# Four-layer graph kernel: intermediates kept in PSUM, bias adds on GpSimd, the diagonal term on VectorE, and a new order of work

## What is computed

```python
# layer 0: attention, 12 heads, masked by adj     layer 3: attention, 12 heads, bias adj, then Wo
# layer 1, twice: h_lin = h @ W_lin.T + b_lin;  ctx = (exp(u)*adj / sum) @ h_lin;  h = relu(ln(ctx))
# layer 2, twice:
a = softmax(h @ h.T / sqrt(D));  delta = a * adj;  attn = delta / (sum(delta) + 1e-10)
hl, hs, hr = h @ wl.T + b_l, h @ ws.T + b_s, h @ wr.T + b_r
ctx = (attn * upper) @ hl + diagonal(attn)[..., None] * hs + (attn * lower) @ hr
h = relu((ctx - mean) / sqrt(var + 1e-12) * g + beta)
```

## Time and profile before

| | |
|---|---|
| median of 3 runs | 2933.51 us (2930.34 to 2935.92) |
| the profiled execution | 2933.42 us, of which the span from first to last instruction is 2931.7 us |
| PE busy | 2823.5 us, 96% |
| DVE busy | 2403.6 us, 82% |
| ACT busy | 1825.3 us, 62% |
| POOL (GpSimd) busy | 1349.7 us, 46% |
| mean granted TensorE clock | 0.988 |
| DMA transposes | 960, 15 per element |

### The profile page before, as it was taken

One profiled execution on the slowest core, in us unless ns is written; L12 is line 12 of the kernel. 1 busy time (PEld: TensorE's weight loads), 2 busy tenths in 40 slices (PEclk: granted clock), 3 DMA queues, 4 the chain that ended last, 5 costly groups with the idle time before them and its releaser, 6 DMA issues.

```text
span 2931.7 us, 93395 instructions
## 1 busy us (share of the span) xinstructions
PE 2823.5 (96%) x35008; PEld 2091.8 (71%) x35008; DVE 2403.6 (82%) x8566; ACT 1825.3 (62%) x4885; POOL 1349.7 (46%) x2571
## 2 busy tenths in 40 slices
PE   6899999999999999999999999999999999999996
PEld 4666767777777777777777777777777777777764
DVE  6867888788888888888888888888888878888767
ACT  5745566566666666666666666666666666665546
POOL 2334454354454454454454454454454445444545
PEclk9899999999999999999999999999999999999997
DMA  9414354344444444444454454444443444544325
GB/s 238 86 30 72 67 101 77 61 84 70 84 86 68 84 85 72 83 86 69 84 84 71 84 84 71 85 84 70 85 84 70 82 77 80 91 79 75 56 39 101
DMA packets 803991, 237.41 MB, mean 81 GB/s; under 512 B 771544, under 2 KB 803416, under 8 KB 803424
## 3 DMA queue, kind: packets, MB, share of 16 engines
q1 hardware_dynamic: 795808, 218.28, 42.3%
q10 hardware_dynamic: 7744, 13.17, 1.4%
HBM read 29.99 MB, written 12.58 MB: 15 GB/s over the span
## 4 chain that ended last, share of the span: by engine, by line
PE 76%; DMA 7%; DVE 6%; ACT 3%; POOL 3%; SPq 2%; issue 2%; ACTq 0%; DVEq 0%; POOLq 0%
PE bank L801 10%; PE bank L802 9%; PE bank L803 9%; PE bank L789 8%; PE bank L790 7%; PE bank L791 7%; PE bank L893 6%; DMA turned<-flat 6%; PE bank L838 4%; PE bank L807 3%; PE bank L886 2%; PE bank L823 2%; PE bank L825 2%; PE bank L824 2%; DVE score L974 2%
## 5 line engine op out<-in xcount | busy, mean ns | idle before, releaser
L789 PE MATMUL bank<-turned,w_hi 128*128 128x128 f16 x4608 | 817.2, 220 | 19.7 <-DMA turned<-flat 17.7
L790 PE MATMUL bank<-turned,w_hi 128*128 128x128 f16 x4608 | 816.4, 220 | 0.0
L791 PE MATMUL bank<-turned,w_lo 128*128 128x128 f16 x4608 | 816.3, 220 | 0.0
L801 PE MATMUL bank<-w_hi,turned 128*128 128x384 f16 x2112 | 692.4, 328 | 23.7 <-DVE w_lo L925 14.2
L802 PE MATMUL bank<-w_lo,turned 128*128 128x384 f16 x2112 | 691.0, 327 | 0.0
L803 PE MATMUL bank<-w_hi,turned 128*128 128x384 f16 x2112 | 690.8, 327 | 0.0
L716 ACT ACTIVATE score<-score,small 128x128 f32<-128x128 f32 x1536 | 500.9, 391 | 152.7 <-DVE small L980 138.0
L707 ACT ACTIVATE ab<-bank 128x384 f16<-128x384 f32 (+1 forms) x768 | 367.0, 484 | 254.3 <-PE bank L791 130.8
L609 POOL TENSOR_TENSOR flat<-score,flat 128x384 f16<-128x384 f32 x256 | 237.2, 927 | 613.6 <-ACT flat L722 613.0
L789 PEld LDWEIGHTS bank<-turned,w_hi 128*128 128x128 f16 x4608 | 453.8, 98 | 51.8 <-DMA turned<-flat 22.4
L790 PEld LDWEIGHTS bank<-turned,w_hi 128*128 128x128 f16 x4608 | 453.9, 99 | 18.6 <-issue 13.1
(11 more groups left out here) (116 smaller groups left out, 6559.0 us busy)
## 6 DMA issues: line engine op xcount, KB each, us to landing
turned<-flat SPq DMA_TRANSPOSE x960, 2.8
x<-x_dram SPq DMA_DIRECT2D x64, 192.0 KB, 2.4
out_dram<-score SPq DMA_DIRECT2D x64, 192.0 KB, 2.2
w_stage<-w_dram ACTq DMA_DIRECT2D x19, 576.0 KB, 5.6
adj<-adj_dram SPq DMA_DIRECT2D x64, 64.0 KB, 2.3
rows<-rows_dram ACTq DMA_DIRECT2D x1, 1920.0 KB, 9.3
turned<-bias_dram SPq DMA_DIRECT2D x4, 9.0 KB
beta<-beta_dram SPq DMA_DIRECT2D x1, 0.5 KB, 6.3
```

The lines of the kernel that those rows point to most:

```text
L789: pe.matmul(dst, lhsT=w_hi[:, w, k, cols], rhs=t_hi[u][:, k, :], start=(k == 0), stop=False)
L790: pe.matmul(dst, lhsT=w_hi[:, w, k, cols], rhs=t_lo[u][:, k, :], start=False, stop=False)
L791: last = pe.matmul(dst, lhsT=w_lo[:, w, k, cols], rhs=t_hi[u][:, k, :], start=False, stop=(k == DT - 1 and w not in BIAS_OF))
L801: pe.matmul(dst, lhsT=t_hi[u][:, k, :], rhs=w_hi[:, w, k, :], start=(k == 0), stop=False)
```

## The change

1. **Biases.** `BIAS_OF` keeps three biases (L0_Q, L0_K, L3_V). The other eight (weights 5, 8 and 9 to 14) are now added by a new POOL part `bias`: after ACT has copied the projection to SBUF, POOL adds a row of `rows` in place. `mix` waits for `biased` instead of ACT's copy.
2. **Diagonal.** `turn_delta` makes only the two triangles, and in an instruction of its own a per-node number, the diagonal. `mix` 2 and 3 issue two matmuls instead of three, and `inner` begins with one more DVE instruction: hs times the diagonal, added into the bank.
3. **PSUM.** `e` of `u_gcn` and `u_di`, and the results of `inner` and `gain`, stay in the PSUM bank in which PE made the product. The banks are handed on only after `delta_gcn`, `delta_di`, `turn` or `residual` has read them.
4. **Small parts.** The `TICK` copies go; `sums` on POOL takes two instructions instead of four.
5. **Memory and start.** The three weight staging tiles now lie in the tiles of the seventh unit, so element 6 is loaded only after all weights are split. `rows` comes in two loads. In `plan()`, the loads of weights 6 to 18 follow parts of ACT (`LOADED_AFTER`; the element that is furthest decides), DMA queues and a slow PE after a pause are part of the model, and transposes are taken to land after 3.60 instead of 3.15 us.
6. **Order.** All urgencies, durations and shifts are new; `PERIOD` is 41.981 instead of 43.452.

```diff
-BIAS_OF = {L0_Q: 0, L0_K: 1, 5: 2, 8: 3, 9: 4, 10: 5, 11: 6, 12: 7, 13: 8, 14: 9, L3_V: 10}
+BIAS_OF = {L0_Q: 0, L0_K: 1, L3_V: 2}
+ROW_OF = {5: 6, 8: 7, **{w: 3 + w for w in range(9, 15)}}
...
-    (PE, "mix", 2): (502.90, 2.010, 2.240, ((VECTOR, "turn_delta", 0), (SCALAR, "project", 9), (SCALAR, "project", 10), (SCALAR, "project", 11)), ()),
+    (PE, "mix", 2): (417.061, 1.340, 1.570, ((VECTOR, "turn_delta", 0), (POOL, "bias", 9), (POOL, "bias", 10), (POOL, "bias", 11)), ()),
...
+LOADED_AFTER = {6: ((SCALAR, "scores", 1),), 7: ((SCALAR, "scores", 2),), 8: ((SCALAR, "scores", 3),), 9: ((SCALAR, "turn", 1),), 10: ((SCALAR, "project", 3),), 11: ((SCALAR, "project", 4),), 12: ((SCALAR, "u_gcn", 0),), 13: ((SCALAR, "turn", 2),), 14: ((SCALAR, "project", 6),), 15: ((SCALAR, "norm", 1),), 16: ((SCALAR, "turn", 3),), 17: ((SCALAR, "u_di", 0),), 18: ((SCALAR, "turn", 4),)}
...
-           "turn_adj": lambda k: (SCALAR, "turn_adj", k), "u_gcn": lambda k: (VECTOR, "u_gcn", k),
-           "u_di": lambda k: (SCALAR, "u_di", k), "turn_delta": lambda k: (VECTOR, "turn_delta", k),
-           "mix": lambda k: (VECTOR, "inner", k)}
+           "turn_adj": lambda k: (SCALAR, "turn_adj", k), "u_gcn": lambda k: (VECTOR, "delta_gcn", k),
+           "u_di": lambda k: (VECTOR, "delta_di", k), "turn_delta": lambda k: (VECTOR, "turn_delta", k),
+           "mix": lambda k: ((VECTOR, "turn", 2), (VECTOR, "residual", 1), (VECTOR, "turn", 4), (VECTOR, "residual", 2))[k]}
...
+        w_stage = [last_unit[:, n * DT * D:(n + 1) * DT * D] for n in range(STAGES)]
...
+            def bias(i, w):
+                u = i % UNITS
+                pool.wait_ge(*proj_hi_done.at(i, "made", w))
...
+                made = proj[u][2 if w < 9 else (w - 9) % 3]
+                pool.tensor_tensor(made, made, rows[:, ROW_OF[w], :], ALU.add).then_inc(biased.of(i), 1)
...
                     for w in L2_W[k - 2]:
-                        pe.wait_ge(*proj_hi_done.at(i, "made", w))
+                        pe.wait_ge(*biased.at(i, "made", w))
                     pe.wait_ge(*mixed_out.at(i, "delta3", k - 2))
-                    for m in range(3):
-                        last = pe.matmul(made[:, 0:D], lhsT=delta3[u][:, m, :], rhs=proj[u][m], start=(m == 0), stop=(m == 2))
-                    last.then_inc(multiplied.of(i), 1)
+                    pe.matmul(made[:, 0:D], lhsT=triangles[u][:, 0, :], rhs=proj[u][0], start=True, stop=False)
+                    pe.matmul(made[:, 0:D], lhsT=triangles[u][:, 1, :], rhs=proj[u][2], start=False, stop=True)\
+                      .then_inc(multiplied.of(i), 1)
...
-                dve.tensor_tensor(delta3[u], bank("turn_delta", layer, i)[:, 0:N].unsqueeze(1).broadcast_to([128, 3, N]), tri[:, :, :], ALU.mult)\
+                dve.tensor_tensor_reduce(out=score[u][:, 2, :], in0=turned, in1=ident, scale=1.0, scalar=0.0, op0=ALU.mult,
+                                         op1=ALU.add, accum_out=col(u, DIAGONAL)).then_inc(numbers.of(i), 1)
+                dve.tensor_tensor(triangles[u], turned.unsqueeze(1).broadcast_to([128, 2, N]), tri[:, 0:2, :], ALU.mult)\
                    .then_inc(mixed_out.of(i), 1)
...
+                if k >= 2:
+                    dve.wait_ge(*numbers.at(i, "diagonal", k - 2))
+                    dve.scalar_tensor_tensor(made[:, 0:D], proj[u][1], col(u, DIAGONAL), made[:, 0:D], ALU.mult, ALU.add)\
+                       .then_inc(numbers.of(i), 1)
...
-                dve.scalar_tensor_tensor(zc[u], made[:, 0:D], mv[u][:, 0:1], rows[:, 2 * k, :], ALU.subtract, ALU.mult)\
+                dve.scalar_tensor_tensor(inner_of(i, k), made[:, 0:D], mv[u][:, 0:1], rows[:, GAIN_ROW[k], :], ALU.subtract, ALU.mult)\
...
-                dve.scalar_tensor_tensor(z[u], zc[u], col(u, GAIN if k < 2 else ROOT), rows[:, 2 * k + 1, :], ALU.mult, ALU.add)\
+                dve.scalar_tensor_tensor(inner_of(i, k), inner_of(i, k), col(u, GAIN if k < 2 else ROOT), rows[:, GAIN_ROW[k] + 1, :], ALU.mult, ALU.add)\
```

More of the change, by code:

```diff
@@ L233 @@
-    (SYNC, "turn", 5): (933.49, 1.240, 3.150, ((POOL, "turn", 5),), ()),
+    (PE, "turn_adj", 0): (0.000, 0.120, 0.380, ((VECTOR, "scores", 3),), ()),
+    (POOL, "turn", 0): (66.763, 0.868, 1.110, ((SCALAR, "turn", 0),), ()),
+    (PE, "mix", 1): (69.466, 0.700, 0.830, ((POOL, "bias", 8), (VECTOR, "delta_gcn", 1)), ()),
+    (POOL, "inner", 1): (73.012, 0.515, 0.765, ((VECTOR, "inner", 1),), ()),
+    (SCALAR, "turn", 0): (103.510, 0.412, 0.707, ((SYNC, "load", 0),), ()),
+    (VECTOR, "gain", 1): (107.515, 0.916, 1.240, ((POOL, "inner", 1),), ()),
@@ new lines @@
+    (POOL, "bias", 5): (478.539, 0.920, 1.200, ((SCALAR, "project", 5),), ()),
+    (PE, "project", 12): (480.991, 1.464, 1.644, ((SYNC, "turn", 4),), ()),
+    (PE, "project", 14): (483.572, 1.464, 1.644, ((SYNC, "turn", 4),), ()),
+    (POOL, "bias", 13): (485.571, 0.920, 1.200, ((SCALAR, "project", 13),), ()),
+    (PE, "scores", 7): (491.204, 0.300, 0.480, ((SCALAR, "scores", 6),), ()),
+    (VECTOR, "gain", 0): (491.504, 0.919, 1.243, ((POOL, "inner", 0),), ()),
+    (POOL, "sums", 0): (493.150, 0.441, 0.662, ((VECTOR, "delta_di", 0),), ()),
@@ L460, in bank, with e_of, inner_of @@
             return pool_of_banks[BANKS_AT[name, k, i][0][n]]
+        def e_of(i, name, layer):
+            return bank(name, layer, i)[:, 0:N]
+        def inner_of(i, k):
+            return bank("mix", k, i)[:, 0:D]
         def across(tile):
```

563 lines of the change are left out of this document (293 added, 270 removed).

## The result

The changed kernel takes 2813.17 us, the median of four runs (2807.87 to 2813.78), against 2934.72 for the kernel before (2930.34 to 2939.37). The ratio is 0.9582, with a 95% interval of 0.9562 to 0.9601. The forecast was 2780 with a range of 2735 to 2850. The direction and the range held; the gain came out as 122 us where 153 was forecast. The profiled execution took 2813.78 us, of which the span is 2812.0.

What follows compares the result with a forecast made beforehand. PE's issue was taken to bound the kernel: 2933.4 us less 166.7 of matmuls is 2766.7, plus 21 of waits in the middle, less 7 at the start, 2780.7, forecast 2780 us. Range 2735 to 2850.

Steps and rivals of the forecast that it cites:

- The work taken off PE: On PE, 512 bias matmuls (83.5 us) and 128 third matmuls of `mix` (83.2 us) go: together 166.7 us less.
- PE is then busy for 2656.8: PE's busy time once the removed matmuls are gone: 2656.8 us, or 41.5 us per element.
- the 20 us kept for that: Allowance on DVE, either way, as no row showed it writing 384 columns to a bank: some 20 us.
- the copies with a result nobody reads ... -52.2 us: On DVE, dropping six one-column copies per element, 384 at 0.136 us, was to save 52.2 us.
- Waits in the middle: PE's idle between 400 and 2800 us was to grow from 31.3 to 52 us, adding 21.
- The rule 6.5 / 3.9: PE's middle idle scales inversely with DVE's room per element, which falls from 6.5 to 3.9 us: 31.3 becomes 52.
- -7: At the start, weights loaded when the first element needs them, against a later element 6: net 7 us less.
- 14.2 are the wait for the first weight, which stays: Of 41.2 us PE idle in the first 150, the first matmul's 14.2 us wait for its weight remains.
- DVE as full as PE: Rival: POOL holds up DVE's instructions with two SBUF operands, 0.33 us each, twelve per element: 2848 us, chance 0.14.
- The L1010 form: Sign on DVE that the forecast is wrong: this instruction's median lies well over 0.293 us.
- Banks run short: Rival: PSUM banks held 4.6 us longer, four times per element, delay each `mix` by 0.25 us: 2845 us, chance 0.07.
- The change doesn't do what it says: Rival: the new order leaves PE waiting for one late element, idle eats the 167 us saved: 2933 us, chance 0.02.

## Why the prediction was right, and where it wasn't

**The sum.** By its own terms it forecast PE busy for 2656.8 us and idle for 122 or 123. Measured are 2675.4 and 136.6: 18.6 and 14 more, together the 33 us by which 2813 lies over 2780.

**The work taken off PE** was counted and priced rightly: the spacing of 0.16 us is still there, and the 148.1 us by which the busy time fell and the 18 us more of slow clock make 166. What failed is the step "PE is then busy for 2656.8", which holds only at the old clock. The clock was never priced for the middle, where some 15 of the 18 us are. They are the largest error.

**DVE** was forecast at 2409 and came to 2423.5, but by errors that cancel: that it is so near is luck. The forecast added lengths of instructions to a busy time in which they overlap. Right were the L1064 form (0.823 to 0.622 with a largest value of 0.627: -51.4 us, forecast -52.0), the triangles (-16.7, forecast -16.9), the diagonal (+46.6, forecast +47.2) and the product (+78.6, forecast +79.4). So an instruction that writes 384 columns to a bank costs the same as one that writes SBUF, and the 20 us kept for that weren't needed. Wrong was "the copies with a result nobody reads ... -52.2 us": they lay in a gap, and the two runs show 9 and 16 us of busy time and none at the end. Also wrong was costing at nothing what reads a bank instead of SBUF: L1076, L1088 and L1144, 128 each, went from 321, 401 and 643 to 280, 280 and 549 ns, 33 us less. L1071 fell from 505 to 385, 15 us, but it reads two operands in SBUF as before and only writes to a bank, so this isn't the bank's: in another run it is at 553. Against it, L1006, L1127, L1141 and L1045 grew by 27, 19, 9 and 6 us.

**POOL** was forecast at 1880 and is at 1748. The adds are 515 us (forecast 530). The two dropped steps of `sums`, costed at nothing, were 42, and POOL's other instructions got shorter too (L598, now L643, from 981 to 942 ns): with the intermediates back in SBUF POOL is busy for 33 us more, so DVE's operands in SBUF hold it up as well. It isn't the bound, as said, and `mix` waits for it for 2.3 us. The adds stand where the trace let them: on POOL they cost 34 us; on PE, beside POOL's, 38. The hold-up of the one line L1127 is worth 17, but by all that POOL does: with small adds its mean is still 252 ns, and how the 17 and the 34 overlap wasn't tried. (With neither it is 2779, and with them only on PE, not tried, some 2817 if the two prices add.)

**Waits in the middle.** I let 31.3 us of idle grow to 52 as DVE's room shrinks; it is 59.8. The direction and the reason hold: waits for transposes are as they were, and the growth is in waits for DVE. The rule 6.5 / 3.9 has no run behind it, so that it came so near is in part luck. The run with small adds shows that POOL's adds take a share, 18.7 us of idle in all with 14.5 of clock; most of the waits that went with them were for transposes, though, and not for DVE.

**Start.** "-7" was wrong: idle in the first 150 us is 43.6, not 34, and the clock there 0.85 for 0.89. The first matmul waits as long as before, but no longer for the weight:

```profile
PE bank L850 <- DMA turned<-flat: 13.7, 1, 13.7
```

The first weight is now split at 9.0 us, where it was 13.9. The transpose of the first x is issued at 7.6 and lands some 6 us later, so it has taken the weight's place as the last to come: "14.2 are the wait for the first weight, which stays" had the time right and missed the cause. The transpose of 10.03 us is indeed shorter, in the chain of waits of the changed kernel:

```profile
34.59 5.25 DMA turned<-flat
```

but PE gained nothing from it: behind the first matmul its waits for transposes in these 150 us rose from 7 to 13 us. Which of late weights and the missing seventh element takes the gain away stays open, as the new plan without loads on demand has as good a start. The tail, left alone in the forecast, has 4 us less of idle.

**The rivals.** "DVE as full as PE" named the right mechanism with the wrong size. It took an excess of 0.33 us for each of twelve instructions, and added it whole to a DVE time that holds the hold-up of before already. Measured (each line's mean less its least value, over L1045, L1061, L1071, L1127, L1141 and L1006), they have 107 us of excess in 768 instructions, or 0.14 each; before it was 63 us, or 0.08. My 0.223 came from L1064, the one line that the order placed worst. It isn't an average property but one of place: L1006 beside a POOL instruction takes its 0.88 in more than half of the elements (median 884 ns; before 352), as one would expect of an order that repeats itself. The L1010 form, named as a sign, has a median of 301 ns, so it shows nothing. The rows of the changed kernel's timeline:

```profile
1007.22 1.00 POOL L643 TENSOR_TENSOR last_unit<-last_unit 128x384 f16<-128x384 f32 x1 [3.10 <-ACT last_unit L754]
...
1007.49 0.88 DVE L1006 SCALAR_TENSOR_TENSOR mask<-adj,minus_beta,mask 128x128 f32<-128x128 f32 x1
```

"Banks run short" is refuted for this order by the two runs in SBUF. "The change doesn't do what it says" got 0.02, with an order that leaves PE waiting. This one was sound in its result but given too little thought: three other plans of the same instructions are at 2906 to 2990. Nothing in the profile of before could tell that the new table would be a good one; the forecast took it for granted. That the order turned out well is the part of the hit that the prediction had no ground for.

**Where the gain is from.** The single edits, each undone in the changed kernel, are worth 60 (diagonal), 38 (bias matmuls), 30 (intermediates in PSUM) and nothing (copies). POOL's adds take 34 back. That makes 94 of the 122 us, if the prices add, which wasn't tried; the rest is put down to the order and the start by what is left over, not by a run.

## What to carry to other kernels

Work taken off a bound engine is worth its length only while the others and the order keep up: here 167 us of matmuls alone brought 70, and with a new order and cheaper forms on DVE 122. When a second engine gets nearly as full as the first, price the granted clock too: 28 us more of idle came with 18 of slow clock, though 62 in the old order came with 5, so look at where the idle gathers. Before moving work to GpSimd, look for VectorE instructions with two SBUF operands, one-column ones too, and give their second operand as a scalar or from a bank.
